# Row masks added with the maximum on VectorE from step 16 on, and experts spread over 40 steps, in a two-layer kernel

## What is computed

```
x = L0_attn_x; xn = layernorm(x)
x = x + attention0(xn) + experts0(xn)        # layer 0, both branches from xn
xn = layernorm(x)
x = x + attention1(xn) + experts1(xn)        # layer 1

attention0: 16 query heads of 16, 4 key/value heads, rotary positions; in windows of 64 tokens
    scores  = q k^T / 4, over the 16 first ("meta") keys and the keys of the last 64 positions
    scores  = where(allowed, scores, -inf)   # causal and in the window, or meta
    y       = softmax(scores) v, then y Wo + bo
experts0:   64 experts, each token takes the best 8; each expert up to 128 tokens,
    out     = (silu(x g) * (x u)) d, weighted and added to the tokens' rows
```

## Time and profile before

| what | value |
|---|---|
| median of 3 runs | 1303.53 us (1303.05 to 1309.62) |
| the profiled execution | 1304.94 us; its span in the trace is 1303.1 us |
| mean granted TensorE clock | 0.989 |
| busy over the span | PE 1245.1 (96%), PEld 1072.7 (82%), DVE 687.3 (53%), ACT 538.6 (41%), POOL 666.8 (51%) |
| layer 0's steps 16 to 63 | 114.4 to 374.5 us |
| first instruction of layer 1 on TensorE | 391.63 us |

### The profile page before, as it was taken

The page is one execution under the profiler, slowest core; times in us unless marked ns, Lnnn a source line. Parts: engine busy times, 40 slices in busy tenths (PEclk is TensorE's granted clock), DMA queues, the critical chain, the costliest instruction groups (busy, mean ns, idle before and its releaser), DMA issues. The chain is left out here.

```text
span 1303.1 us, 21647 instructions
## 1 busy us (share of the span) xinstructions
PE 1245.1 (96%) x7842; PEld 1072.7 (82%) x7877; DVE 687.3 (53%) x1429; ACT 538.6 (41%) x1193; POOL 666.8 (51%) x523
## 2 busy tenths in 40 slices
PE   7598999999989998999999999999999998999999
PEld 6477888878857887888788888888888887899988
DVE  6985555455667677675654435434434334432235
ACT  4675566665555333334333334333343333211121
POOL 4646777775203565666667655666646552011110
PEclk9799999999999999999999999999999999999999
DMA  8624878886705210111221111211111102799931
GB/s 310 170 54 108 180 175 188 177 173 125 177 2 174 70 62 32 61 66 49 82 65 62 39 63 58 65 53 37 54 53 37 37 25 72 278 344 333 328 124 65
DMA packets 112697, 150.70 MB, mean 116 GB/s; under 512 B 12144, under 2 KB 94192, under 8 KB 112464
## 3 DMA queue, kind: packets, MB, share of 16 engines
q1 hardware_dynamic: 96320, 123.21, 29.4%
q0 software_dynamic: 16272, 26.10, 10.4%
HBM read 121.31 MB, written 27.97 MB: 115 GB/s over the span
## 5 line engine op out<-in xcount | busy, mean ns | idle before, releaser
L1646 PE MATMUL a_p_p<-a_xr,a_wr 128*128 128x512 f32 x1152 | 308.7, 403 | 2.4 <-DVE g_x L2206 2.4
L1646 PEld LDWEIGHTS a_p_p<-a_xr,a_wr 128*128 128x128 f32 x1152 | 206.6, 189 | 42.6 <-DVE g_x L2206 3.1
L1973 POOL TENSOR_TENSOR a_sqsum<-a_sqsum,a_sq 128x512 f32<-128x512 f32 x60 | 78.0, 1299 | 230.7 <-ACT a_sq L1855 230.7
L1941 POOL TENSOR_TENSOR a_wr<-g_hold,a_wr 128x768 fp32r<-128x768 f32 x63 | 122.3, 1942 | 18.6 <-DVE a_wr L2005 18.6
L2041 DVE SCALAR_TENSOR_TENSOR a_gated<-a_th,a_p_o 128x512 f32<-128x512 f32 x64 | 44.0, 687 | 158.7 <-ACT a_sq L1855 158.7
L412 POOL DMA_INDIRECT acc<-l_ye,g_slot_token x64 | 102.4, 1601 | 39.9 <-ACT l_ye L780 20.7
L1975 POOL TENSOR_TENSOR a_gr<-a_gated,a_gr 128x512 fp32r<-128x512 f32 x64 | 97.9, 1529 | 23.6 <-DVE a_gr L2045 23.6
L1659 PE MATMUL a_p_p<-a_wvr,a_xr 128*128 128x512 f32 x384 | 104.6, 408 | 1.0 <-DVE a_xr L1999 1.0
L1717 PE MATMUL a_p_w<-a_gr,l_wo_r 128*128 128x512 f32 x384 | 100.7, 397 | 0.3 <-POOL a_gr L1975 0.3
L1828 ACT ACTIVATE a_qk<-a_p_p 128x512 f32<-128x512 f32 x64 | 38.2, 598 | 140.8 <-PE a_p_p L1646 140.8
L1701 PE MATMUL a_p_o<-a_sc,a_v 128*128 128x128 f32 x512 | 89.2, 276 | 6.6 <-DVE a_sc L2021 6.6
(11 more groups left out here) (292 smaller groups left out, 2796.2 us busy)
## 6 DMA issues: line engine op xcount, KB each, us to landing
g_hold<-in_Wqkg SPq DMA_DIRECT2D x64, 384.0 KB, 3.2
e_up<-in_gate_up SPq DMA_DIRECT2D x23, 1024.0 KB
g_hold<-in_gate_up SPq DMA_DIRECT2D x64, 192.0 KB
e_down<-in_down SPq DMA_DIRECT2D x23, 512.0 KB, 5.6
g_hold<-in_Wv SPq DMA_DIRECT2D x16, 512.0 KB, 4.4
l_down<-in_down SPq DMA_DIRECT2D x64, 96.0 KB
acc<-l_zero SPq DMA_DIRECT2D x2, 2176.0 KB, 12.5
rows<-l_zero SPq DMA_DIRECT2D x1, 2955.5 KB, 26.5
```

Of the source, the lines that this page charges most:

```text
L1646: mm = pe.matmul(dst[:, :], wr[n % 2][:, wp, kk, c * P:(c + 1) * P], xr[n // H1 % 2][:, xp, kk, :], start=(kk, xp, wp) == (0, 0, 0), stop= ...
L1941: pool.tensor_tensor(wr[n % 2][:, 1, :, :], w[n % 2], wr[n % 2][:, 0, :, :], ALU.subtract).then_inc(w_parts, 1)
L1973: pool.tensor_tensor(sqsum[b % 2][:, :], sqsum[b % 2][:, :], sq[a % 2][:, :], ALU.add).then_inc(summed, 1)
```

## The change

`ADDED = 4 * G0` is step 16. From there on `score` issues no mask product, and the first score product of a bank starts it anew. VectorE adds the mask to one head's 208 scores and takes the running maximum in one call (`tensor_tensor_reduce`), four per step; the masked scores go to `masked`, which nothing reads. The mask in a bank is the same tile as before. In the ticks' table tick k stands in step 15 + 3k // 5 (2, 2, 1, 2, 2, 1, ... ticks) in place of 15 + k // 2, so that the 66 ticks end in step 54 and not in step 47.

```
+    ADDED = 4 * G0
+        masked = [m.sb(f"masked{r}", [P, KEYS0], BF16) for r in range(R0)]
...
-        ticks_at = {n: [k for k in range(TICKS) if TICK0 + k // 2 == n] for n in range(FIRST, LAST)}
+        ticks_at = {n: [k for k in range(TICKS) if TICK0 + 3 * k // 5 == n] for n in range(FIRST, LAST)}
...
                     bank = p_s[pp % 2]
-                    pe.matmul(bank[:, :, 0:KEYS0], identb[:, :], mask[:, kind(t), :, :], start=True, stop=False,
-                              skip_group_check=True)
+                    if n < ADDED:
+                        pe.matmul(bank[:, :, 0:KEYS0], identb[:, :], mask[:, kind(t), :, :], start=True, stop=False,
+                                  skip_group_check=True)
                     for i in range(2):
                         mm = pe.matmul(bank[:, i, 0:KEYS0], qT[t % 3][:, kv // 2, 2 * c + i, :], kz[:, kv, t % TPB, :],
-                                       start=False, stop=True, skip_group_check=True)
+                                       start=n >= ADDED, stop=True, skip_group_check=True)
...
                     dve.wait_ge(scored, pp + 1)
-                    dve.tensor_reduce(top[n % 3][:, 2 * c:2 * c + 2], p_s[pp % 2][:, :, 0:KEYS0], AX_X, ALU.max).then_inc(max_done, 1)
+                    if n < ADDED:
+                        dve.tensor_reduce(top[n % 3][:, 2 * c:2 * c + 2], p_s[pp % 2][:, :, 0:KEYS0], AX_X, ALU.max).then_inc(max_done, 1)
+                        continue
+                    if n == ADDED:
+                        dve.wait_ge(rounded, ROUNDED)
+                    dve.wait_ge(max_done, pp - 1)
+                    for i in range(2):
+                        r = 2 * c + i
+                        ins = dve.tensor_tensor_reduce(masked[r][:, :], p_s[pp % 2][:, i, 0:KEYS0], mask[:, kind(n // G0), 0, :], 1.0,
+                                                       2.0 * MASKED, ALU.add, ALU.max, top[n % 3][:, r:r + 1])
+                    ins.then_inc(max_done, 1)
```

## The result

The changed kernel takes 1311.39 us (median of 9 runs, 1309.19 to 1314.67), the kernel before 1305.61 beside it (9 runs): ratio 1.0041, 95% interval 1.0027 to 1.0054. One of the nine before, 1782.59 us, is a slow run and counts neither in the ratio nor in its interval. The change costs about 0.4%, which is inside the 0.5% that I had called hard to tell from no change, but its interval excludes 1. The time is 1.4 us above the upper end of my range and 8.9 above the forecast; 2.1 of that is the kernel before itself, which stood at 1303.53 when I predicted.

The account below looks back on a forecast made before the run. TensorE, handing one chain to and fro with VectorE, was taken as the bound. Step 55 4.6 us earlier let the combine gain 2.5; the tail lost 1.4: -1.1 in all, 1302.5 us, range 1294 to 1310.

Parts of the forecast that it names:

- Removed from TensorE, 0.37 us per step: Layer 0, steps 16 to 63: dropping 96 mask products saves TensorE 0.185 us per bank, 0.37 per step.
- Added on VectorE, D = 0.63: VectorE's step grows by D: four new maximum pairs at 0.435 us, 1.74, replace two reductions taking 1.11.
- Rivals 2 and 3: Dearer VectorE pairs: no overlap, 0.515 us, 1307.3 (chance 0.13); as dear as a whole reduction, 1311.3 (chance 0.12).
- rival 3: VectorE's pair is as dear as a whole reduction, 0.58 us, D = 1.21: 1311.3 us, chance 0.12.
- What stands behind this: TensorE's waits for VectorE's hT in layer 0 grow 1.25 us per four steps, 12.2 over steps 16 to 54.
- Step 55 at 344.7: Step 55 of layer 0 starts 4.6 us earlier, at 344.7: 14.4 saved, 12.2 given back, 2.4 filled.
- Spreading fills 2.4 us: Moving expert ticks into steps 48 to 54 fills 2.4 us of idle TensorE.
- Last scatter 3.3 us ahead of step 55: GpSimd's last scatter in layer 0 comes 3.3 us before step 55, at 341.4, where it was 325.99.
- The sum 19.2 us behind the last scatter; the combine waits: End of layer 0: sum lands at 360.6, so VectorE, ready at 360.0, waits and combines 2.5 us earlier than before.
- Rival 4: The sum's transfers are late by more; no reason seen, no separate size or chance, counted within the forecast.
- Tail +1.4: Behind the first combine, four more maxima on a full VectorE cost 2.5 us, 1.1 absorbed by idle time: 1.4 lost.
- Rival 1: TensorE is the bound and the new waits don't come: 13.2 us faster, 1290.3, chance 0.20.

Follow-up runs that it names:

- e10: The changed kernel run again unchanged, beside the kernel before on one chip: ratio 1.0031.
- e9: The kernel before run again unchanged, as a control: ratio 1.0011 to the kernel before.
- e15: Kernel before with masks off TensorE from step 16, experts two per step, VectorE keeping its old plain reduction on unmasked scores: ratio 0.9975.
- e2: Kernel before with only the experts' ticks spread, five in three steps, masks staying on TensorE: ratio 1.0022.
- e8: e7 with the experts' ticks spread nine in five steps, against the kernel before: ratio 0.9942.
- e11: e7 with the experts' ticks spread five in three steps, against the kernel before: ratio 0.9976.
- e7: Changed kernel with experts back at two per step, ScalarE's two copies and VectorE's diagonal behind the step's first tick: ratio 0.9948 to the kernel before.
- e12: Changed kernel with SyncE loading layer 1's first weights only after the four sums land: ratio 0.9978 to the kernel before.
- e13: e11 with layer 1's first weights loaded only after the sums, as in e12: ratio 0.9929 to the kernel before.

## Why the prediction was wrong

- **What bounds the kernel.** Right in part. TensorE and VectorE do hand a chain to and fro, but I followed one link of it. L613 (after: L616) is a link as well: it had 2.2 us of waits for ye in the view of before and 5.7 by the starts in steps 19 to 43 alone, at 27 of 48 places, more than L596 with its 2.7, and my sum left them out. The small wait of before is the one that grew most when the engine was made faster.
- **Removed from TensorE, 0.37 us per step.** A little too much. Where nothing is waited for, the way from the first score product to the expert's product falls from 0.80 to 0.50, by 0.30 us; behind a projection (steps 4i+3) the way from the projection's last product falls from 1.10 to 0.75, by 0.35. Over 39 steps that is 12.2 us and not 14.4.
- **Added on VectorE, D = 0.63.** Wrong: 0.19. The first half I had at 0.295 with its overlap, and so it is; the second half costs nothing. Rivals 2 and 3, which rest on a dearer pair, fall with it; that rival 3 named 1311.3 us and 1311.39 came is luck, since its pair of 0.58 us is twice the measured one. The Trainium skill's section named in the prediction (VectorE: DVE Perf Modes, "The DRAIN you can't avoid") lets an instruction that is not held start earlier, and the rows with 0.295 between starts and 0.37 of duration agree with that: I had weighed the rule without its exception.
- **What stands behind this: new waits of 1.25 us per four steps, all for hT.** This is the step that failed: the wait for ye was put at nothing. By the starts, from step 16 to 55, the waits ahead of `expert_turn` (ye) grow by 8.0 us (e10 against e9: 6.4) and those ahead of `expert_out` (hT) by 5.2 (5.1). By my own slope D = 0.19 would have made some 0.8 of new waits per four steps, 7.9 us in all, all of them at hT. In sum 13.2 (11.5) came, close to the 12.2 of the forecast, and that is luck: the part for ye that I left out and the part for D that I had too large nearly cancel. e15 shows that VectorE's price isn't what brings them: at D = 0 the waits grow by 9.0 us and 2.0 of 10.9 are left.
- **Step 55 at 344.7.** 348.88. The trace of after begins step 16 1.0 us earlier, and from there on the way is 0.5 us longer than before (e10 against e9: 1.2 shorter) where 4.6 less was forecast: the saving is 2.2 us smaller than assumed, spreading gave 1.2 us at most, and the new waits are about as large as forecast, for the reason above.
- **Spreading fills 2.4 us.** Wrong for this kernel: 0.2 us in e2. With the copies and the diagonal moved it is 1.0 in e8 and 2.1 in e11, against e7; single traces differ by up to 1.5.
- **Last scatter 3.3 us ahead of step 55.** 2.2 measured. Together with step 55 it made the scatter 5.3 us late against the forecast.
- **The sum 19.2 us behind the last scatter; the combine waits.** Right: 19.5. Rival 4, still later transfers, did not come; e12 shows that they need not take so long. The combine waits, but 4.1 us where I had 0.6, since step 55 and the scatter were late.
- **Tail +1.4.** +1.0 behind the combine, but not for the reason given: with D = 0.19 the four maxima there add 0.8 at most. That TensorE goes idle in front of it and comes back at a lower clock was not in the sum: from the first combine to the last sum e10 takes 27.05 us, with the clock at 0.50 for 5 us of it, and e12, with the clock at 1.00, 24.58.
- **Rival 1** (TensorE is the bound, 1290.3, chance 0.20) is the furthest from what came.
- **The time.** Layer 0 ends 5.2 us later than forecast: 4.2 for step 55, 1.1 for the scatter's place, and little behind them. The kernel before was 2.1 us slower beside the changed one than in the runs that I started from.

So most of the relieved engine's saving went to two suppliers that were hardly ahead of it, and the loss on top comes from a chain of transfers that had 17.9 us in hand and starts 20.7 us later. What stays open: why the last scatter comes 2.2 us ahead of step 55 and not 3.3, how much of e13's gain over e8, if any, is real, and what holds ScalarE's first `th` in some traces.

## What to carry to other kernels

Before an engine is relieved, list every wait that it has already, small ones above all, and ask of each how much earlier the supplier could be. Read the waits from the distances between starts, since a view that counts from modelled ends hides the short ones. The gain can't be more than the least of these rooms, and each mend (here a copy or a diagonal set behind what is waited for) brings the next link to light. Work spread towards the end of a stage moves the stage's last transfer with it: add its whole way (issue, loads, landing, and what shares the queues) before counting what spreading fills. A load that nobody needs yet can wait for the transfer that somebody does.

## What the runs showed of the hardware

- The sum with a running maximum over 128x208 (f32 from PSUM and bf16) is listed with 0.37 us and takes 0.295 from start to start; the 0.08 us read of the maximum behind it is hidden by the next one.
- The same accumulating transfers took 11.1 to 14.8 us beside the loads of layer 1's weights and 7.4 to 11.2 without them.
- After 5.65 us of idle TensorE (e10) the granted clock was 0.50 over the next 5 us (1.2 GHz); after 1.87 us (e12) it stayed 1.00 (2.4 GHz). The four score products behind the combine took 1.34 us at the lower level and 1.06 at the upper; both contain a wait for the maxima between the two banks, without which four take 0.66 to 0.72 at the upper. The way from the first combine to the last sum was 27.05 - 24.58 = 2.5 us longer in e10 than in e12; how much of that is the clock alone was not tried.
